# A macaron transformer block in float32: the attention stage's bank for the last row maxima, the place of GpSimd's sum of probabilities, and the queue that sends the denominators

## The reference

```
x = x + 0.5 * ffn(layernorm(x))     # top 2 of 8 experts with a capacity, plus 2 shared experts
x = x + attention(layernorm(x))     # 16 heads of 64, rotary + Fourier position terms
x = x + 0.5 * ffn(layernorm(x))     # the same weights again
```

## Time and profile before

| | us |
|---|---|
| median of 3 runs | 1308.43 (1307.06 to 1311.01) |
| the profiled execution's own time | 1307.98 |
| its span in the trace | 1306.2 |

### The profile page before, as it was taken

One profiled execution on the slowest core, in us unless ns is written; L12 is line 12 of the kernel. 1 busy time (PEld: TensorE's weight loads), 2 busy tenths in 40 slices (PEclk: granted clock), 3 DMA queues, 4 the chain that ended last, 5 costly groups with the idle time before them and its releaser, 6 DMA issues.

```text
span 1306.2 us, 20886 instructions
## 1 busy us (share of the span) xinstructions
PE 1241.4 (95%) x7346; PEld 773.3 (59%) x7346; DVE 945.5 (72%) x1443; ACT 628.0 (48%) x917; POOL 934.0 (72%) x652
## 2 busy tenths in 40 slices
PE   5999999799999999999999999999999998999998
PEld 3666656456556565555655656565656555666665
DVE  6656777778878887877878788778877775665632
ACT  3444522464555545446455545555555543433422
POOL 0543447688899898888889999989989861443343
PEclk9999999999999999999999999999999999999999
DMA  5353040122323232232232323232323220443140
GB/s 166 129 178 126 5 147 17 42 58 52 72 50 72 53 70 55 54 65 56 61 64 59 65 52 73 50 74 50 72 52 75 50 42 10 146 138 91 57 154 17
DMA packets 118678, 95.35 MB, mean 73 GB/s; under 512 B 75760, under 2 KB 85008, under 8 KB 118320
## 3 DMA queue, kind: packets, MB, share of 16 engines
q1 hardware_dynamic: 118576, 94.01, 29.2%
HBM read 57.53 MB, written 2.88 MB: 46 GB/s over the span
## 4 chain that ended last, share of the span: by engine, by line
PE 41%; POOL 40%; issue 11%; DVE 5%; DMA 1%; ACT 1%; SPq 0%; POOLq 0%; DVEq 0%; ACTq 0%
PE banks L453 15%; POOL work L1412 12%; POOL qk_l L1407 10%; PE banks L466 9%; POOL turn L1402 8%; POOL turn L1396 5%; PE banks L1145 5%; PE banks L1127 4%; POOL o_t L1419 4%; PE banks L988 2%; PE banks L1161 2%; PE banks L1132 1%; POOL x_tok L1427 1%; PE banks L1068 1%; PE banks L415 1%
## 5 line engine op out<-in xcount | busy, mean ns | idle before, releaser
L1000 DVE TENSOR_REDUCE neg_max<-banks 128x2 f32<-128x1024 f32 x256 | 305.3, 1226 | 94.6 <-PE banks L988 92.8
L1242 ACT ACTIVATE work<-banks 128x1024 f32<-128x1024 f32 x256 | 262.5, 1027 | 91.3 <-PE banks L1132 79.9
L1145 PE MATMUL banks<-work 128*64 128x512 f32 x1024 | 233.8, 598 | 1.1 <-ACT work L1242 1.1
L1402 POOL TENSOR_TENSOR turn<-turn,side_turned 128x512 f32<-128x512 f32 x128 | 162.9, 1293 | 58.1 <-DMA side_turned<-side 57.8
L1407 POOL TENSOR_TENSOR qk_l<-turn,qk_h 128x512 fp32r<-128x512 f32 x128 | 199.4, 1559 | 3.5 <-ACT qk_h L977 3.3
L1412 POOL TENSOR_TENSOR work<-work 128x1024 f32<-128x1024 f32 x64 | 163.3, 2552 | 34.2 <-PE banks L1145 33.9
L1396 POOL TENSOR_TENSOR turn<-turn,fenc 128x512 f32<-128x512 f32 x128 | 162.8, 1293 | 14.0 <-DVE side L1311 13.8
L1145 PEld LDWEIGHTS banks<-work 128*64 128x64 f32 x1024 | 67.8, 136 | 134.0 <-issue 110.1
L807 POOL TENSOR_TENSOR o_raw<-o_raw,work 128x512 f32<-128x512 f32 x52 | 67.0, 1289 | 89.7 <-DVE o_raw L723 89.6
L807 POOL TENSOR_TENSOR work<-work 128x512 f32<-128x512 f32 x44 | 56.6, 1291 | 95.2 <-DVE work L723 52.1
L1332 DVE TENSOR_TENSOR work<-work 128x1024 f32<-128x1024 f32 x64 | 108.2, 1690 | 11.2 <-PE banks L1145 11.2
(11 more groups left out here) (177 smaller groups left out, 2470.7 us busy)
## 6 DMA issues: line engine op xcount, KB each, us to landing
work<-share SPq DMA_DIRECT2D x32, 1024.0 KB, 9.3
side_turned<-side SPq DMA_DIRECT2D x256, 128.0 KB, 3.1
rec_all<-rec_d SPq DMA_DIRECT2D x128, 128.0 KB, 3.0
x_tok<-in_x SPq DMA_DIRECT2D x8, 256.0 KB, 5.8
out<-x_tok SPq DMA_DIRECT2D x8, 256.0 KB, 9.2
work<-in_w_gate_up SPq DMA_DIRECT2D x1, 1280.0 KB, 7.9
work<-in_w_qk SPq DMA_DIRECT2D x1, 1024.0 KB, 9.6
den_d<-den_rows SPq DMA_DIRECT2D x64, 4.0 KB
```

Source lines behind the costliest of these rows:

```text
L1000: return nc.vector.tensor_reduce(neg_max[:, g % 2, qt::DH], of, AX.X, ALU.max, negate=True)
L1145: ins = nc.tensor.matmul(O[OWN[h], :], v_all[:, kt, n * DH:(n + 1) * DH], pt[:, g % 2, kt, h * T:(h + 1) * T], start=(kt == 0), stop=(kt = ...
L1242: nc.scalar.activation(pt[:, g % 2, kt, :], S[kt].rearrange("p h q -> p (h q)"), ACT.Exp, scale=QSCALE).then_inc(s["probs"], 1)
L1402: nc.gpsimd.tensor_tensor(turn[:, g % 2, part], turn[:, g % 2, part], side_turned[:, part], ALU.add).then_inc(done, 1)
```

## The change

Four edits, all in the attention stage:

1. The denominators' DMA to DRAM is issued by ACT behind its own copy, not by SP. SP now waits for it to land, and then reads back as before.
2. POOL does `second_sum` ahead of the low part of k, not behind it.
3. The fourth part of the maxima goes to OW, and stands on PE between `scores(p, 0)` and `scores(p, 1)`, not behind both; it waits only for the second part to have been read.
4. The values' product goes to bank 4 (the first of M2) for all groups but the last three, and `copy_o` reads it there. It waits for three parts of the next group's maxima to be read. A new wait keeps the first part of the maxima behind `copy_o`.

```
-            M = (M2, OW, M2, M2)
+            M = (M2, OW, M2, OW)
+            def own_bank(g):
+                return g < N - 3
+            def o_bank(g):
+                return bank[4] if own_bank(g) else O
...
                     else:
-                        pe.wait_ge(s["maxes"], g * TT + (0, 0, 1, 3)[qt])
+                        pe.wait_ge(s["maxes"], g * TT + (0, 0, 1, 2)[qt])
+                    if qt == 0:
+                        at_least(pe, s["o_copied"], g - 2)
                     maxima_products(g, qt, M[qt])
...
                         pe.wait_ge(s["v_ready"], min(g + TT, B * 2 * TT))
-                        pe.wait_ge(s["maxes"], min((g + 2) * TT + 2, N * TT))
+                        if own_bank(g):
+                            pe.wait_ge(s["maxes"], (g + 2) * TT + 3)
+                        else:
+                            pe.wait_ge(s["maxes"], min((g + 3) * TT, N * TT))
+                            pe.wait_ge(s["y_done"], g - 2)
                         at_least(pe, s["o_copied"], g)
-                        at_least(pe, s["y_done"], g - 2)
                     for h in range(2):
                         n = 2 * (g % PAIRS) + h
-                        ins = nc.tensor.matmul(O[OWN[h], :], v_all[:, kt, n * DH:(n + 1) * DH],
+                        ins = nc.tensor.matmul(o_bank(g)[OWN[h], :], v_all[:, kt, n * DH:(n + 1) * DH],
...
                     if exists(last):
                         scores(p, 0)
-                    scores(p, 1)
+                    else:
+                        scores(p, 1)
                     if exists(nxt):
                         maxima(nxt, 3)
+                    if exists(last):
+                        scores(p, 1)
...
-                    nc.scalar.activation(o_raw[:, g % 2], O, ACT.Copy).then_inc(s["o_copied"], 1)
+                    nc.scalar.activation(o_raw[:, g % 2], o_bank(g), ACT.Copy).then_inc(s["o_copied"], 1)
...
                     nc.scalar.activation(den_rows[:, 0:HALF], W[:, 0:HALF], ACT.Copy).then_inc(s["den_copied"], 1)
+                    act.wait_ge(s["den_copied"], g + 1)
+                    act.dma_start(den_d[g], den_rows[0:P:32, 0:HALF]).then_inc(s["den_out"], 16)
...
-                    if exists(ahead):
-                        low(ahead, K, s["k_high"])
                     if exists(p - 1):
                         second_sum(p - 1)
                     if exists(ahead):
+                        low(ahead, K, s["k_high"])
                         low(ahead, Q, s["q_high"]).then_inc(s["low"], 1)
...
                 def den_in(g):
-                    sp.wait_ge(s["den_copied"], g + 1)
+                    sp.wait_ge(s["den_out"], 16 * (g + 1))
                     at_least(sp, s["rec_ready"], g)
-                    sp.dma_start(den_d[g], den_rows[0:P:32, 0:HALF]).then_inc(s["den_out"], 16)
-                    sp.wait_ge(s["den_out"], 16 * (g + 1))
```

## The result

The changed kernel took 1274.38 us (median of 4 runs, 1271.32 to 1275.40), the kernel before 1307.74 beside it (1305.35 to 1311.01): a ratio of 0.9739, 95% interval 0.9712 to 0.9767. That is 33.4 us faster; 1278.4 was forecast.

What follows compares the result with a forecast made beforehand. PE, at 95% of the span, was taken as the bound, waiting for POOL's late sum. From 1307.98 us, −25.8 − 10.2 + 6 = −30.0 gave 1278.0, as a median 1278.4; range 1270 to 1295.

Steps and rivals of the forecast that it cites:

- POOL's sum ahead of the low part of k: On POOL: the sum ends at 11.18, before the denominators can start at 11.88, so PE's wait goes; −25.8 us.
- The 29.2: On PE: loss from POOL's late sum, 13.37 − 12.88 = 0.49 us a period over 60; 3.4 us taken off as work.
- The order on PE: On PE: the fourth maxima between the scores' tiles saves 0.17 us a period of waiting for ACT; 10.2 us over 60.
- The values' product in bank 4: On PE: same matmuls at the same cost, no new wait; frees bank 6 for the fourth maxima; worth nothing itself.
- The DMA from ACT: On ACT: an issue of 0.52 us fits into 0.94 idle, no cost; DVE's reciprocals can go about 1.8 us earlier.
- Left over: On DVE: small statistics and norm steps make some first sums still meet POOL's sum; 6 us left for that.
- The sum: Whole kernel: −25.8 − 10.2 + 6 = −30.0 us, to 1278.0, as a median 1278.4; chance 0.60.
- Rival 1: On PE: the stall moves to the maxima's product or `scores(p, 0)`, the 10 us are missing, 1288.6; chance 0.12.
- Rival 2: On the port DVE and POOL share: POOL's sum holds DVE's first sum, 2.2 us too long; 1288 to 1308; chance 0.08.
- Rival 3: On ACT: wait and issue exceed 0.94 us, delaying the exponentials; at 1.42 all gain is gone; chance 0.12.
- the 1.3 of the extreme: On ACT: its issue stands behind SP's four, leaving it 1.3 us too late; 1360 us.
- Rival 4: On POOL: its instructions stretch against DVE's and the denominators still wait; 1300 us; chance 0.08.

Runs made afterwards that it cites:

- den_only: The kernel before with only the denominators' DMA moved to ACT's queue: 1299.6 us, ratio 0.9952.
- banks_only: The kernel before with only the banks and the place of the fourth maxima changed: 1302.3 us, ratio 0.9976 to the kernel before.
- order_undone: The changed kernel with the fourth maxima behind `scores(p, 1)` again, in its new bank: 1281.9 us, ratio 0.9815 to the kernel before.
- sum_late: The changed kernel with DVE's first sum released by the whole values' product instead of its first half: 1301.9 us, ratio 0.9967 to the kernel before.
- act_three: The changed kernel with two more DMAs of the denominators' rows from ACT, to DRAM nobody reads: 1325.0 us, ratio 1.0147 to the kernel before.
- pool_only: The kernel before with only POOL's sum moved ahead of the low part of k: 1283.8 us, ratio 0.9834.
- act_two: The changed kernel with one more DMA of the denominators' rows from ACT, to DRAM nobody reads: 1290.3 us, ratio 0.9877 to the kernel before.

## Why the prediction was right

By its own steps:

- *POOL's sum ahead of the low part of k, −25.8 us.* Right in mechanism and near in size: 22.8 us alone, and 0.9912 − 0.9739 = 0.0173 of 1307, 22.6 us, as the last of the edits. The 29.2 that it started from were not all one thing: the three long periods have 7.8 of them over 12.88, and these also go by the DMA alone (den_only). The sum ends at 11.07, forecast at 11.18; the low parts no longer meet DVE's sum. POOL did not become the bound: in the changed kernel it has 1.1 us idle ahead of the sum.
- *The order on PE, −10.2 us.* Right in mechanism, a little too large: 0.13 a period and not 0.17, 7.8 us. `scores(p, 1)` hands over to the values' product in 0.35, where the maxima did in 0.33, so from the last product of `scores(p, 0)` to the values' product 0.15 is saved (1.51 against 1.66); the other 0.02 are lost in the rest of the period. The order is worth its price only once the wait for POOL is gone; with that wait in place (banks_only) no change is inside the interval.
- *The values' product in bank 4, nothing.* Right for the 61 groups that it applies to; what it enables is the order. For the last three it isn't used, and they wait for four reduces instead of two: once, in period 62, PE idles 0.84 us until the fourth is done.
- *The DMA from ACT, no cost.* Right: 0.48 against 0.52 assumed, the exponentials start 1.47 into the period as before. What it brings was said too large in its first step: the read back is issued 3.83 us into the period instead of 5.05, 1.2 earlier and not 1.8, because landing took 3.27 us (425.12 to 428.39) and not the 2.65 of the earlier trace rows; that SP's four transfers beside it are the reason is likely, but wasn't tested. Over the 60 periods the median goes from 4.76 to 3.81. Alone the edit is worth 6 us, as one of several ways to be rid of the long periods; on top of the others it is 3.9 us of the traces.
- *Left over, +6 us.* This was the term furthest off: three periods with 0.35 to 0.48 too much, 1.2 us. DVE's first sum starts ahead of POOL's in every period of the trace, but in those three by 0.15, 0.13 and 0.03 us only. That it is POOL that is held in all three is luck of a few hundredths; with DVE held in one, order_undone lost 2.8 us.
- *The sum.* The periods fell by 33.0 us where 30.0 were forecast. The order was 2.4 too large and what is left over 4.8 too large, and the two errors go opposite ways, so a part of the closeness is luck as well.
- *Rival 1*: the stall did not move. *Rival 2*, the port lock, is a real mechanism (order_undone, sum_late) that the change just misses. It is near: with the first sum released 1.8 us later it costs 26 us by the traces and 28 to 30 by the times, of 33, though POOL is then the one that is held. *Rival 3* has its price right: act_three is the case in which it decides, 0.78 us late, between the break-even of 0.48 that was worked out and the 1.3 of the extreme. Its cause as told, an ACT issue behind SP's, doesn't occur. Its argument that SP's issue times barely vary holds for the denominators' DMA (0.52 to 0.58 in the kernel before), not for the four of side (0.46 to 1.81). *Rival 4* falls.
- Not foreseen: what comes behind the 60 periods, 2.9 us longer. The two stalls in period 62 are 2.8 (the first is in pool_only too; before, PE came there later and had waited 1.79 us at the denominators of period 61 instead of 0.74). The clock isn't the reason: its mean over this stretch is 0.98 in both kernels.

## What to carry to other kernels

An in-order engine that makes others wait should do first what is waited for soonest, even if it must idle for it: 1.1 us of idle time on POOL in each period bought 0.4 us on the engine that bounds. Look at edits as a set: saving time on the bounding engine in front of a wait is worth little until the wait goes, and several edits that each only move a side chain forward can share one benefit. Where an instruction of one engine is held while another's runs, as DVE's and POOL's hold each other here, compare the starts of the two rather than their lengths; 0.03 us decided who was held. And look for small steps ahead of the large one: held, a step of 8 columns cost as much as a sum of 1024.

## What the runs showed of the hardware

- A DMA of the denominators issued by ACT takes 0.48 us of its queue when it stands alone, and 0.49 to 0.75, half of them below 0.58, behind another of its own (act_two, act_three); while SP issued four others, it was no longer. One of 64 took 1.05.
- Two sums released by one event, DVE's 0.04 to 0.12 us ahead: DVE's ran at its own length (1.22 to 1.25), and POOL's took 3.36 to 3.43 instead of 2.41, in all 60 periods (sum_late). With POOL's 0.11 ahead, DVE's took 3.38 instead of 1.2 (order_undone).
- A DVE step on 128x8 with inputs in SBUF took 1.20 us beside POOL's turned parts and 0.17 behind them.
- Around the same idle time of 2.5 us on PE the mean granted clock of 9 us was 0.62 in one execution and 1.00 in another. Over whole executions of one kernel the mean varied from 0.995 to 1.000.
